# A four-layer graph network in groups of four graphs: the first two groups and the last two run side by side

## The reference

```python
x = layernorm(x + L0(x, adj))   # attention: w = adj * exp(q k^T), rows divided by their sum, w @ v
x = layernorm(x + L1(x, adj))   # GCN: three times adj @ (x W) + b, relu after the first two
x = layernorm(x + L2(x, adj))   # hypergraph: H = adj != 0; relu(conv(x, W1)), norm, conv(., W2), + x
x = layernorm(x + L3(x, adj))   # 8-head attention, scores * mask, softmax, @ v, Wo
# conv(x, W) = D^-1 H B^-1 H^T (x W^T) + b, D and B the degrees of nodes and hyperedges
# mask = adj + adj
```

## Time and profile before

| what | us |
|---|---|
| median of 3 executions | 1046.44 |
| lowest and highest | 1045.45, 1046.67 |
| span of the profiled execution | 1044.3 |
| TensorE busy (matmuls) | 1010.7 |
| VectorE busy | 840.8 |
| ScalarE busy | 642.8 |
| GpSimd busy | 491.3 |

### The profile page before, as it was taken

The page is one execution under the profiler, slowest core; times in us unless marked ns, Lnnn a source line. Parts: engine busy times, 40 slices in busy tenths (PEclk is TensorE's granted clock), DMA queues, the critical chain, the costliest instruction groups (busy, mean ns, idle before and its releaser), DMA issues.

```text
span 1044.3 us, 21534 instructions
## 1 busy us (share of the span) xinstructions
PE 1010.7 (97%) x8292; PEld 901.9 (86%) x8292; DVE 840.8 (81%) x2246; ACT 642.8 (62%) x1739; POOL 491.3 (47%) x298
## 2 busy tenths in 40 slices
PE   9799999999999999999999999999999999998876
PEld 7689898988989898898989889898988989897664
DVE  5666978788897878889787888978788897878666
ACT  4454946749385674938567493856749385673724
POOL 2244274547444454744445474444547444342613
PEclk8999999999999999999999999999999999999998
DMA  6110100102010010101001010100101010000001
GB/s 235 38 51 11 52 2 32 61 12 62 21 62 11 24 59 11 62 22 61 12 21 62 11 62 21 61 12 23 61 12 61 21 62 11 22 2 11 22 1 41
DMA packets 15078, 39.14 MB, mean 37 GB/s; under 512 B 1792, under 2 KB 1792, under 8 KB 14848
## 3 DMA queue, kind: packets, MB, share of 16 engines
q1 hardware_dynamic: 14976, 37.77, 10.3%
HBM read 29.38 MB, written 8.39 MB: 36 GB/s over the span
## 4 chain that ended last, share of the span: by engine, by line
PE 91%; DVE 4%; ACT 2%; issue 1%; POOL 1%; DMA 0%; POOLq 0%; DVEq 0%; SPq 0%
PE ps L465 83%; PE ps L775 5%; PE ps L716 1%; DVE pr L1236 1%; PE ps L702 1%; PE ps L646 1%; DVE mx L1241 1%; ACT pr L935 1%; DMA pr<-in_weights 0%; DVE x L1120 0%; POOL pr L1368 0%; DVE st L1058 0%; POOL rstd L1322 0%; DVE den L1250 0%; ACT up_high L912 0%
## 5 line engine op out<-in xcount | busy, mean ns | idle before, releaser
L1368 POOL TENSOR_TENSOR pr<-pr,den 128x1024 f32<-128x1024 f32 x64 | 132.0, 2064 | 68.7 <-DVE den L1256 68.5
L935 ACT ACTIVATE pr<-pr,mx 128x128 f32<-128x128 f32 x384 | 149.3, 407 | 6.6 <-DVE mx L1241 6.6
L1322 POOL TENSOR_TENSOR rstd<-var,neg_half 128x4 f32<-128x4 f32 (+1 forms) x84 | 74.4, 886 | 96.5 <-DVE var L1069 94.8
L1347 POOL TENSOR_TENSOR x<-x,rows 128x1024 f32<-128x1024 f32 x16 | 38.0, 2376 | 169.4 <-PE ps L465 169.4
L1074 DVE TENSOR_SCALAR x<-x,mv,rstd 128x256 f32<-128x256 f32 x256 | 90.5, 414 | 23.1 <-POOL rstd L1322 23.1
L1357 POOL TENSOR_TENSOR hv<-hv,neg_half 128x2 f32<-128x2 f32 x32 | 22.4, 701 | 161.8 <-DVE hv L1202 161.8
L1058 DVE BATCH_NORM_STATS2 st<-x 128x6 f32<-128x256 f32 x256 | 92.6, 412 | 1.9
L1236 DVE TENSOR_TENSOR pr<-ps,adjB 128x1024 f32<-128x1024 f32 x64 | 75.4, 1219 | 13.9 <-PE ps L465 13.9
L935 ACT ACTIVATION_READ_ACCUMULATOR pr<-pr,mx 128x1 f32 x384 | 78.8, 205 | 0.0
L929 ACT ACTIVATE qkT<-ps,biases 128x512 f32<-128x512 f32 x64 | 39.7, 689 | 62.7 <-PE ps L465 62.4
L1352 POOL TENSOR_TENSOR up_rest<-upT,up_high 128x1024 fp32r<-128x1024 f32 x32 | 77.7, 2430 | 0.0
(11 more groups left out here) (196 smaller groups left out, 3248.8 us busy)
## 6 DMA issues: line engine op xcount, KB each, us to landing
xT<-in_xT SPq DMA_DIRECT2D x16, 512.0 KB, 5.0
x<-in_x SPq DMA_DIRECT2D x16, 512.0 KB, 3.7
out_x<-x SPq DMA_DIRECT2D x32, 256.0 KB, 2.0
adjT<-in_adjT SPq DMA_DIRECT2D x16, 256.0 KB, 5.2
adjB<-in_adj SPq DMA_DIRECT2D x16, 256.0 KB, 5.0
pr<-in_weights SPq DMA_DIRECT2D x2, 512.0 KB, 6.0
...
```

Of the source, the lines that this page charges most:

```text
L935: act.activation(pr[:, b, k, :], pr[:, b, k, :], ACT.Exp, bias=mx[:, b, k:k + 1], accum_out=den[:, b, 0, k:k + 1]).then_inc(exp_ready, 1)
L1322: pool.tensor_tensor(rstd[i][:, bs], var[i][:, bs], neg_half[:, bs], ALU.pow).then_inc(rstd_ready[i], len(pairs))
L1368: pool.tensor_tensor(pr[:, b], pr[:, b], den[:, b, 1, :].unsqueeze(2).broadcast_to([P, HEADS, P]), ALU.mult).then_inc(pr_ready, 1)
```

## The change

PROLOGUE, SCHEDULE and EPILOGUE are written anew.

- The prologue runs stage A of groups 0 and 1 in turns, then B and C as before. The epilogue runs stages B and C of groups 14 and 15 in turns.
- The loop runs from T0 = 4 to NG - 2, 11 passes. A pass may hold steps of four groups: N is the group after A's, T the one before it, whose stage A ends in the pass (BACK below).
- Group 1 in stage A and group 15 in stages B and C have tiles of their own (`..._b`, `..._z`), laid over tiles that are not in use then, and other PSUM banks (low(), up4()). gm and p0T are gone (the results go into hT and e0); gmT exists twice.
- keep_busy goes from twelve steps to two, both behind set_vec.
- The initial loads come in another order, with xT and x of group 1 added; the first adjB is loaded after two gram_turn steps.
- Waits on banks and tiles are given by small tables (`due`); some are gone, others are at other steps.
- On VectorE, set_reps and incidence come before rest_att; in the loop x1_norm comes between degrees and gram_scale, mha_shift3 before x0_norm, and incidence, att_exp, att_out and x0's steps stand at the end of the pass, for the next group.

```diff
 PROLOGUE = {
-    "PE": [("keep_busy2", 0), ("keep_busy5", 0), ("set_att", 0), ("set_vec", 0), ("att_t", 0), ("att_t_rest", 0),
...
+    "PE": [("set_att", 0), ("set_vec", 0), ("keep_busy2", 0), ("att_t", 0), ("att_t_rest", 0), ("keep_busy5", 0),
+        ("set_down", 0), ("set_wo", 0), ("att_scores", 0), ("att_v0", 0), ("att_v1", 0), ("att_t", 1), ("att_v0", 1),
+        ("att_out", 0), ("att_t_rest", 1), ("att_v1", 1), ("gram", 0), ("att_scores", 1), ("gcn_ax", 0), ("att_out", 1),
...
-    "DVE": [("set_rep", 0), ("set_att", 0), ("rest_att", 0), ("set_vec", 0), ("rest_Wv0T", 0), ("set_reps", 0),
-        ("incidence", 0), ("rest_W2", 0), ("rest_WupT", 0), ("set_down", 0), ("rest_Wv3T", 0), ("att_exp", 0),
...
+    "DVE": [("set_rep", 0), ("set_reps", 0), ("set_att", 0), ("incidence", 0), ("rest_att", 0), ("set_vec", 0),
+        ("rest_Wv0T", 0), ("rest_W3", 0), ("set_down", 0), ("set_wo", 0), ("incidence", 1), ("att_exp", 0),
...
 SCHEDULE = {
...
-        ("C", "mha_div0"), ("A", "att_out"), ("A", "att_res1"), ("B", "hyper_rest0"), ("B", "hyper_rest1"),
-        ("C", "mha_div1"), ("A", "x0_means0"), ("A", "x0_means1"), ("A", "x0_stats"), ("C", "mha_max3"),
-        ("A", "degrees"), ("A", "x0_norm"), ("C", "mha_div2"), ("C", "mha_shift3"), ("A", "gram_scale"),
...
+    "DVE": [("A", "degrees"), ("T", "x1_norm"), ("A", "gram_scale"), ("C", "mha_div2"), ("C", "mha_turn1"),
...
+        ("B", "mha_scores1"), ("B", "mha_div0"), ("B", "mha_max2"), ("N", "att_exp"), ("B", "mha_max3"),
+        ("N", "att_out"), ("T", "hyper_rest0"), ("T", "hyper_rest1"), ("B", "mha_div1"), ("N", "att_res1"),
+        ("N", "x0_means0"), ("N", "x0_means1"), ("N", "x0_stats"), ("B", "mha_shift3"), ("N", "x0_norm")],
...
+    "POOL": [("A", "x0_stats"), ("C", "mha_div2"), ("B", "up_rest0"), ("C", "mha_div3"), ("B", "up_rest1"),
+        ("A", "x0_bias"), ("N", "x_rest"), ("N", "att_t"), ("B", "hyper_down0"), ("C", "x3_stats0"), ("C", "x3_stats1"),
+        ("B", "hyper_down1"), ("B", "x2_stats"), ("B", "x2_bias"), ("B", "mha_div0"), ("T", "x1_bias"),
+        ("A", "x1_stats"), ("B", "mha_div1")],
...
 EPILOGUE = {
...
-        ("mha_wo1", 2), ("hyper_down1_high", 1), ("hyper_down1", 1), ("hyper_out", 1), ("keep_busy8", 1),
-        ("keep_busy5", 1), ("keep_busy7", 1), ("keep_busy0", 1), ("mha_xt", 1), ("mha_qk01", 1), ("mha_qk01_rest", 1),
...
+        ("hyper_down1", 1), ("mha_xt", 2), ("mha_qk01", 2), ("mha_qk01_rest", 2), ("mha_qk2", 2), ("mha_qk3", 2),
+        ("mha_scores0", 2), ("hyper_out", 1), ("mha_scores1", 2), ("mha_xt", 1), ("mha_qk01", 1), ("mha_v0", 2),
+        ("mha_v1", 2), ("mha_turn0", 2), ("mha_qk01_rest", 1), ("mha_qk2", 1), ("mha_qk3", 1), ("mha_turn1", 2),
+        ("mha_scores0", 1), ("mha_ctx0", 2), ("mha_wo0_high", 2), ("mha_turn2", 2), ("mha_scores1", 1), ("mha_wo0", 2),
+        ("mha_v0", 1), ("mha_v1", 1), ("mha_turn3", 2), ("mha_turn0", 1), ("mha_ctx1", 2), ("mha_turn1", 1),
...
+T0, T1 = 4, 1
...
+BACK = {"N": -1, "A": 0, "T": 1, "B": 2, "C": 3}
...
+        def low(g):
+            return 4 if begun(g) else 0
+
+        def up4(g):
+            return 0 if ended(g) else 4
...
+            sp.dma_start(xT_b[:], A["xT"][1]).then_inc(xT1_in, 16)
             sp.dma_start(pr_flat[:, d:d + width(IN_PR)], columns("W1", "W2")).then_inc(w12_in, 16)
+            sp.dma_start(x_b[:], A["x"][1]).then_inc(x1_in, 16)
+            sp.dma_start(adjT[1][:], A["adjT"][1]).then_inc(adjT_in[1], 16)
...
-            sp.dma_start(adjB[:], A["adj"][0]).then_inc(adjB_in, 16)
-            sp.dma_start(adjT[1][:], A["adjT"][1]).then_inc(adjT_in[1], 16)
+
+            def first_adjB(g):
+                sp.wait_ge(gmT_done, 2)
+                sp.dma_start(adjB[:], A["adj"][0]).then_inc(adjB_in, 16)
...
-                if pair == 0 and not first(g):
-                    dve.wait_ge(out_stored, 32 * g)
+                due = {(0, 15): 0}.get((pair, g), {0: 16 * g}.get(pair, 0))
+                if due > 0:
+                    dve.wait_ge(out_stored[0], due)
```

More of the change, by code:

```diff
@@ L253, in build, with over @@
     with ctx:
+        home, ends = {}, [(nc.sbuf_base + P - 1) // P * P, nc.sbuf_usable_end // 32 * 32]
+        def over(name, shape, at_byte, dtype=F32):
+            return nc.alloc_sbuf_tensor_at(name, shape, dtype, offset=at_byte)
         def sb(name, shape, dtype=F32):
-            return ctx.enter_context(nc.sbuf_tensor(name, shape, dtype))
+            size = (4 * math.prod(shape[1:]) + 31) // 32 * 32
+            if size % P:
+                ends[1] -= size
+                home[name] = ends[1]
+            else:
+                home[name] = ends[0]
+                ends[0] += size
+            assert ends[0] <= ends[1]
+            return over(name, shape, home[name], dtype)
         def sem(name):
@@ L376, in run @@
                 steps[name](g)
-            for t in range(3, NG - 1):
+            for t in range(T0, NG - T1):
                 for stage, name in SCHEDULE[who]:
-                    steps[name](t - "ABC".index(stage))
+                    steps[name](t - BACK[stage])
             for name, back in EPILOGUE[who]:
@@ L396, in final, with begun, ended, before @@
             return isinstance(g, int) and g == NG - 1
+        def begun(g):
+            return int(g == 1)
+        def ended(g):
+            return int(g == NG - 1)
+        def before(g):
+            return 0 if g == 2 else g - 1
+        def low(g):
+            return 4 if begun(g) else 0
+        def up4(g):
+            return 0 if ended(g) else 4
+        def x_of(g):
+            return x_b if begun(g) else x
+        def xT_of(g):
+            return xT_b if begun(g) else xT
+        def xT_high_of(g):
+            return xT_high_b if begun(g) else xT_high
@@ new lines, in up_high_of, with up_rest_of, upT_of, sqs_of @@
+        def up_high_of(g):
+            return up_high_z if ended(g) else up_high
+        def up_rest_of(g):
+            return up_rest_z if ended(g) else up_rest
+        def upT_of(g):
+            return upT_z if ended(g) else upT
+        def sqs_of(g):
+            return sqs_z if ended(g) else sqs
+        def y2_of(g):
+            return y2_z if ended(g) else y2
+        def pr_of(g):
+            return pr_z if ended(g) else pr
+        def qkT_of(g):
+            return qkT_z if ended(g) else qkT
@@ new lines, in v3_of, with v3_bank, adjB_of, x3_of @@
+        def v3_of(g):
+            return v3_z if ended(g) else v3
+        def v3_bank(g):
+            return 6 if g == NG - 2 else 2
+        def adjB_of(g):
+            return adjB_z if ended(g) else adjB
+        def x3_of(g):
+            return x3_z if ended(g) else x3
+        def ctxT_of(g):
+            return ctxT_z if ended(g) else ctxT
+        def ctx_rest_of(g):
+            return ctx_rest_z if ended(g) else ctx_rest
+        def norm(i, g):
+            return i + 4 if (begun(g) if i < 2 else ended(g)) else i
@@ L493, in keep_busy @@
                 for _ in range(4):
-                    mm(ps[:, 7 if g < 3 else 1, :], fill[:, 0:P], fill[:])
+                    if first(g):
+                        mm(ps[:, 7, :], fill[:, 0:P], fill[:])
+                    else:
+                        mm(ps[:, 1, :], high["WupT"][:, 0, 0:P], high["WupT"][:, 0, :])
             def set_att(g):
@@ L1078, in x0_means @@
                 dve.wait_ge(res0_ready, GB * g + 2 * pair + 2)
[L1079 removed]
+                means(0, g, pair, x0_of(g))
             def x1_means(g, pair):
@@ L1230, in mha_scores @@
                 dve.wait_ge(s3h_done, 2 * g + pair + 1)
-                if pair == 0:
+                if pair == 0 and ended(g):
+                    dve.wait_ge(adjZ_in, 16)
+                elif pair == 0:
                     dve.wait_ge(adjB_in, 16 * g + 16)
```

543 lines of the change are left out of this document (335 added, 208 removed), and 321 rows, old and new, of tables (EPILOGUE, PROLOGUE, SCHEDULE).

## The result

The changed kernel takes 1078.89 us (median of 4 runs, 1076.56 to 1079.74) against 1046.41 of the kernel before: ratio 1.031, 95% interval 1.029 to 1.032. It is slower by 32.5 us where 18.5 us less were predicted.

A forecast was written before the change was run, and what follows sets the result against it. TensorE was taken as the bound, busy 97% of the span. Sixteen groups at loop pace 974.4, start 23.4, end 26.9 and loop 1.1 gave a span of 1025.8; plus 2.1, 1027.9 us, range 1013 to 1041.

The forecast's parts named there:

- The loop: 11 loop passes: gram_scale slightly later on VectorE, 0.1 us a pass taken, 1.1 us in all (0 to 4.4).
- the price of an overlap: VectorE beside GpSimd: 0.9 us per overlap on VectorE, worth nothing in the loop, one or two counted within the ends' waits.
- that rule: Shared port lock of VectorE and GpSimd: three overlaps fewer in the last 50 us would give 2.7 us less, 1025.2.
- Rival (d): Loop: x1_norm ahead of gram_scale makes gcn_1 wait, 2.2 us a pass, 1051 in all; chance 0.06.
- The start: Before the loop: two groups fill each other's gaps, overhead 23.4 us instead of 29.5 (range 19 to 28).
- the 5.0 us of waits: Before the loop: what remains of 9.1 us of TensorE waits once group 1's steps fill group 0's gaps.
- The end: After the loop: groups 14 and 15 side by side, overhead 26.9 us instead of 40.4 (22.3 to 34).
- 5.4 us of waits: End, until group 14's masked scores: three TensorE waits of 1.7, 1.5 and 2.2 us.
- the 55.5 of the sum: End, from group 14's masked scores: VectorE bounds it, 48.5 us of work, 4.6 of waits, 2.4 for the last store.
- Rival (b): End: without filler the clock falls and short bursts add 10 to 12 us, 1038 to 1040; chance 0.12.
- the main case: Both ends gain as summed, loop 0 to 4.4 us, whole 1018 to 1039; chance 0.72.
- 9.9 us of filler: Old end: keep_busy matmuls with their gaps, counted as part of the 40.4 us of overhead there.

The follow-up runs named there:

- e6: Changed kernel with its loop reordered so that four meetings of VectorE and GpSimd operations are gone, x1_norm moved too: 1046.17 us.
- e3: Changed kernel with x1_norm behind gram_scale instead of before it in the loop: 1078.94 us.
- e7: Changed kernel with two VectorE prologue places altered, rest_att before incidence and rest_WoT ahead of group 2's residual: 1073.99 us.
- e10: Changed kernel with e6's loop, e7's prologue, e8's filler, both fillers at the very front and square_sum0(14) behind group 13's turns: 1035.11 us.
- e12: Kernel of e6 with the eight maxima of groups 14 and 15 taken over 4 of 128 columns: 1042.84 us.
- e11: Kernel before the change without the eight keep_busy steps of its epilogue: 1054.65 us, ratio 1.0075.
- e8: Changed kernel with sixteen filler matmuls put before mha_xt(15): 1077.72 us.
- e2: Changed kernel with, in the loop, square_sum0 behind x3_stats0 and GpSimd's x_rest and att_t behind hyper_down1: 1066.90 us.
- e13: Kernel of e6 with square_sum0 put back before mha_wo0 in the loop: 1055.79 us.

## Why the prediction was wrong

*The loop (predicted 1.1, measured 29.6).* This is the step that failed: the loop term, bounded at 0 to 0.4 us a pass and taken as 0.1, measured 2.7 a pass. It looked at the right place: gcn_ax and gcn_1 behind x0_norm and gram_scale. But it booked "shift3 now runs while GpSimd computes rstd" as time won. The shift reads two tiles in SBUF, and the rstd beside it took 1.85 instead of 1.02, on the one path that had 0.4 us of slack. And it said of the price of an overlap, 0.9 us, that "in the loop both lie under TensorE and are worth nothing". With VectorE busy 51 of 60.9 us and an operation of TensorE queued behind nearly each of its results, that isn't so: with four meetings of 0.8 to 1.2 us each a pass grew by 2.7 us, and e6, without them, has lost that again. The row that should have warned is mha_div2's 2.77 against 1.90: it was known how long a blocked operation gets, and not asked which pairs the new orders bring together. Placing both engines' lists beside each other, with the durations of the kernel before, would have been the way to look for the squares beside up_rest1 and x0_bias.

The Trainium skill, "SBUF — State Buffer", section "Who interferes with whom", says that the engine that issues first holds the shared pair for the whole instruction and that the other fully blocks. By that, as an estimate, the later operation takes what is left of the earlier one and then its own time: 1.97, 1.68, 2.56 and 2.01 us for the 1.83, 1.56, 2.43 and 1.85 above, which agree to within 0.2 us. The prediction priced that rule at 2.7 us in the end, beside its sum, and at nothing in the loop.

*Rival (d)* (slower, by a longer pass, deciding from 1.8 us) had the side, the place and nearly the size of the pass (2.2 guessed, 2.7 measured), but by luck: its mechanism, x1_norm's queue, was worth 0.4 of it by e3. Its 1051 also kept the gains of the ends, which did not come. It had a chance of 0.06.

*The start (23.4, measured 31.4).* att_t, put at 12.8, came at 14.43. incidence took 4.5 us, not 2.2: its first and last operations met GpSimd's xT_rest and its addition to x (1.19 and 2.17 instead of 0.41 and 0.69). VectorE, then TensorE:

```profile
9.25 1.19 DVE L1407 TENSOR_SCALAR hT<-adjT 128x512 f32<-128x512 f32 x1
...
11.60 2.17 DVE L1416 TENSOR_TENSOR bhT<-hT,cnt 128x512 f32<-128x512 f32 x1
13.70 0.68 DVE L1295 TENSOR_TENSOR att_rest<-upT,att_high 128x512 fp32r<-128x512 f32 x1
```

```profile
14.43 0.80 PE L638 MATMUL ps<-xT_high,att_high 128*128 128x512 f32 x1 [2.38 <-DVE att_rest L1295]
```

The prediction had moved rest_att's 1.59 unchanged, but incidence took over the meeting (rest_att itself 0.68). Of the 5.0 us of waits the sum left, one alone was 5.4, and no row of the kernel before could show it:

```profile
92.40 0.76 PE L638 MATMUL ps<-fT_high,WupT_high 128*128 128x512 f32 x1 [5.39 <-DVE WoT_rest L1295]
```

hyper_up01(0) waits for the rest part of WoT, which stands behind gram_scale(2) in VectorE's new list; half clock follows. That was to be read from the tables and wasn't. It is worth the 5 us of e7, in which att_t came no earlier. The loads' new order was not costed; e10 shows 3.3 us of it (the later landing) once the rest is out of the way.

*The end (26.9, measured 41.2).* Before group 14's masks the sum had 5.4 us of waits; there were 12.2, and with gaps and slower matmuls about 16. TensorE's waits behind the loop in the changed kernel:

```profile
PE ps L947 <- DVE x L1322: 4.7, 1, 4.7
PE ps L638 <- DVE x L1322: 2.9, 1, 2.9
PE ps L638 <- DVE pr L1513: 2.7, 1, 2.7
PE ps L638 <- DVE pr L1486: 2.4, 3, 0.9
```

The 2.9 (x0_norm of 15) falls to 1.4 with the loop's fix (e6) and the 2.7 (copies of group 13's turns) to 0.8 with e10: meetings again, this time a sum of squares that took 2.75 us. From the masks of group 14 on, the kernel took 59.2 us (1017.4 to 1076.6), 3.7 more than the 55.5 of the sum, so that part was nearly right in size. Its reason was only half right, as e12 shows: VectorE's sum is not alone the bound here; the clock is in it. The clock in the middle of it:

```profile
1008.00:1032.00 24.00, 16.57 (x119) 12.61 (x119) 20.71 (x52) 12.77 (x49) 4.31 (x4) 0.80 0.00 1
1022.60:1032.60 10.00, 6.21 (x20) 5.00 (x21) 9.76 (x22) 9.15 (x45) 3.71 (x3) 0.51 0.00 0
```

That stretch, from the first mask on, in the changed kernel and in e10, whose orders there differ by the filler alone:

```profile
1017.39:1076.60 59.21, 43.30 (x428) 35.80 (x428) 47.69 (x98) 32.83 (x120) 22.81 (x16) 0.86 0.07 28
```

```profile
977.18:1032.80 55.62, 43.24 (x444) 35.08 (x444) 47.63 (x98) 32.60 (x120) 22.80 (x16) 0.97 0.08 29
```

With VectorE's work unchanged and the clock up, it takes the 55.6 us of the sum's 55.5. So the 3.7 us on top fit the clock, for which the sum had 0.5.

The whole end divides so, by the prediction's own count at loop pace. Before: TensorE idle 23.3, filler 9.0, bias 2.1, and 5.9 by which matmuls ran longer than in the loop. The prediction's list had no entry for these 5.9 and 22.5 of waits and gaps, where the trace has 17.3 before its last matmul. Changed: idle 28.2, bias 2.1, and 10.9 of longer matmuls. Running the groups side by side took the filler out, but it brought 4.9 us more idle time and 5.0 more of slow matmuls.

*Rival (b)* (filler and clock): e11 shows that the filler was worth 8 us in the old epilogue. With two groups side by side the runs differ: no clear gain in e8, and up to 3.8 us in e10, where the clock did not fall until the last matmul. So dropping it cost something in the new order too, and the main case was too sure that it costs little. The gain of the side-by-side end had to pay for the old filler's 8 us first, while the sum had booked 9.9 us of filler as overhead that goes away.

What stays open: the 21.9 us that TensorE still idles in e10's end were not taken apart further. Of the four meetings only the squares' were taken out with a gain of their own (e2), and one of them put back (e13); the meetings of rstd and att_exp were removed with profit only together with the rest (e6). What filler is worth in the new end wants more than e8's one run. Why a pass of e6 is 0.1 us below the 60.9 of the kernel before was not tested. Whether the side-by-side prologue alone, with the old epilogue, would be better than e10 was not tried.
